# A graph network's gathers: row-by-row loads for one tile of every eighth step instead of every fourth

## The reference

```python
src, dst = (edge_index[0], edge_index[1])
h = node_features @ enc_W + enc_b
for l in range(N_LAYERS):
    cat = jnp.concatenate([h[src], h[dst], edge_features], axis=-1)
    m = jax.nn.relu(cat @ msg_W1[l] + msg_b1[l]) @ msg_W2[l] + msg_b2[l]
    agg = jax.ops.segment_sum(m, dst, num_segments=n_nodes)
    h = _gru_cell(agg, h, gru_Wih[l], gru_Whh[l], gru_bih[l], gru_bhh[l])
return jax.nn.relu(h @ ro_W1 + ro_b1) @ ro_W2 + ro_b2
```

## Time and profile before

| | |
|---|---|
| device time, median of 3 plain runs | 6155.57 us (6152.11 to 6167.82) |
| span of the one profiled execution | 9775.6 us |
| instructions recorded in it | 72,182 |
| granted TensorE clock, mean | 0.571 |
| GpSimd busy | 4639.2 us, 47% of the span |
| VectorE busy | 3532.6 us, 36% |
| TensorE busy (matmuls) | 2880.1 us, 29% |
| ScalarE busy | 346.4 us, 4% |

### The profile page before, as it was taken

How to read it: one execution, slowest core, us unless ns; L and a number is a source line. 1 busy time by engine, 2 the same in 40 slices (tenths; PEclk the granted TensorE clock), 3 DMA queues, 4 the chain that set the end, 5 groups by cost and what they waited for, 6 DMA issues and landing times.

```text
span 9775.6 us, 72182 instructions
## 1 busy us (share of the span) xinstructions
PE 2880.1 (29%) x7290; PEld 1610.2 (16%) x7290; DVE 3532.6 (36%) x4656; ACT 346.4 (4%) x542; POOL 4639.2 (47%) x4865
## 2 busy tenths in 40 slices
PE   3323322322322332222222222223232222322223
PEld 2111111111111221111111111112111111111112
DVE  2333333333333433333333333333333334333334
ACT  0000000000000000000000000000000000000001
POOL 5444444444444454444444444445454445545543
PEclk6555555555555555555555555555555555555555
DMA  3111111111111111111111111111111111111111
GB/s 87 31 31 30 30 30 30 28 31 30 31 30 30 30 28 30 30 30 30 30 30 29 30 30 27 30 31 30 30 31 31 30 30 34 31 31 31 31 30 25
DMA packets 351443, 308.63 MB, mean 32 GB/s; under 512 B 149364, under 2 KB 237518, under 8 KB 350568
## 3 DMA queue, kind: packets, MB, share of 16 engines
q0 software_dynamic: 155328, 159.79, 8.6%
q1 hardware_dynamic: 118271, 110.17, 4.0%
q10 hardware_dynamic: 77328, 33.96, 1.4%
HBM read 280.52 MB, written 22.83 MB: 31 GB/s over the span
## 4 chain that ended last, share of the span: by engine, by line
SPq 57%; issue 38%; DVE 2%; PE 1%; another core or an unknown queue 1%; DMA 0%; ACT 0%; POOL 0%; DVEq 0%; ACTq 0%; POOLq 0%
SPq L473 46%; SPq L469 6%; SPq L642 2%; SPq L633 1%; SPq L527 1%; DVE work_ps L1493 1%; SPq L630 1%; DVE folds L1528 0%; DVE p_src L1490 0%; PE bank L838 0%; DMA p_src<-p_tab 0%; PE work_ps L949 0%; PE bank L962 0%; SPq L662 0%
## 5 line engine op out<-in xcount | busy, mean ns | idle before, releaser
L798 POOL DMA_INDIRECT p_src<-p_tab,idx_all x4767 | 4551.1, 955 | 4916.8 <-DVE work_ps L1493 3467.4
L962 PE MATMUL bank<-hot,folds 128*128 128x96 f32 x2496 | 660.1, 413 | 4012.9 <-issue 2053.0
L1490 DVE TENSOR_TENSOR p_src<-work_ps,p_src 128x512 f32<-128x512 f32 x624 | 427.6, 685 | 3374.9 <-DMA p_src<-p_tab 2912.1
L962 PEld LDWEIGHTS bank<-hot,folds 128*128 128x128 f32 x2496 | 532.1, 296 | 4278.5 <-issue 2198.0
L949 PE MATMUL work_ps<-w_edges,msg 128*128 128x512 f32 x1248 | 1120.0, 997 | 21.4 <-DMA windows_sb<-q_tab 21.4
L1523 DVE SCALAR_TENSOR_TENSOR work_ps<-work_ps,rel 128x1024 f32<-128x1024 f32 x624 | 768.8, 1232 | 21.5
L1493 DVE TENSOR_TENSOR work_ps<-p_src,bank 128x1024 f32<-128x1024 f32 x624 | 767.0, 1229 | 21.4
L1528 DVE TENSOR_REDUCE folds<-work_ps 128x256 f32<-128x1024 f32 x624 | 758.4, 1215 | 0.0
L959 PE MATMUL bank<-hot,counts 128*34 128x96 bf16 x416 | 68.9, 261 | 2248.6 <-issue 1278.6
L1538 DVE TENSOR_TENSOR sums<-bank,sums 128x96 f32 x624 | 158.1, 253 | 872.6 <-remote 699.5
L959 PEld LDWEIGHTS bank<-hot,counts 128*34 128x34 bf16 x416 | 27.1, 108 | 2368.2 <-issue 1359.8
(11 more groups left out here) (167 smaller groups left out, 1800.9 us busy)
## 6 DMA issues: line engine op xcount, KB each, us to landing
p_src<-p_tab ACTq DMA_DIRECT2D x9792, 0.2 KB
p_src<-p_tab SPq DMA_DIRECT2D x9792, 0.2 KB
p_src<-p_tab,idx_all POOLq DMA_INDIRECT x4830
msg<-in_edge_k SPq DMA_DIRECT2D x156, 256.0 KB
pick<-rel_tab SPq DMA_DIRECT2D x312, 96.0 KB
windows_sb<-q_tab ACTq DMA_DIRECT2D x312, 24.0 KB
windows_sb<-q_tab SPq DMA_DIRECT2D x312, 24.0 KB
pick<-q_tab ACTq DMA_DIRECT2D x312, 24.0 KB
```

The costliest lines, as they stand in the source:

```text
L798: pool.indirect_dma_start(out=p_src[r][0:rows, t, :], out_offset=None, in_=p_tab[l][0:NODES, :], in_offset=bass.IndirectOffsetOnAxis(ap=id ...
L962: last = nc.tensor.matmul(fold_ps, folds[:, b, :], hot_all[n % 2][:, s * BLOCKS + b, 1:WINDOW + 1], start=(b == 0), stop=(b == BLOCKS - 1))
L1490: nc.vector.tensor_tensor(rows, edge_ps[k % 2], rows, ALU.add).then_inc(with_edge, 1)
```

## The change

The singles are now the eighth tile of every eighth step, 25 in a layer instead of 51; GpSimd gathers the other 26. SyncE issues 32 of the 64 rows ahead of the inputs of one group and the other 32 ahead of the next group's, each in two loads of sixteen offsets. ScalarE issues pieces of eight rows, each with its own load of eight offsets, from six steps ahead (two pieces) to one step ahead of the tile's own. The landing semaphores are two for each queue instead of four. The list of single nodes and its offsets shrink from 52 to 26 rows.

```diff
-PIECES = 4
-AHEAD_OF = 5
+PERIOD = 2 * GROUP
+PIECES = 8
+AHEAD_OF = 6
 PIECE = (128 - SP_ROWS) // PIECES
-SINGLE_SEMS = 4
-SINGLES = GROUPS - 1
+SINGLE_SEMS = 2
+SINGLES = STEPS // PERIOD - 1
...
         def has_singles(m):
-            return m % GROUP == GROUP - 1 and m // GROUP < SINGLES
+            return m % PERIOD == PERIOD - 1 and m // PERIOD < SINGLES
...
         def single_rows(eng, kind, l, m, first, n, landed):
-            for at in range(first, first + n, PIECE):
-                here = offsets[m // GROUP:m // GROUP + 1, at:at + PIECE]
+            each = min(n, 16)
+            for at in range(first, first + n, each):
+                here = offsets[m // PERIOD:m // PERIOD + 1, at:at + each]
...
         def pieces_at(m):
-            due = [(m + AHEAD_OF - q, q) for q in range(PIECES)]
-            if m == 0:
-                due = [(GROUP - 1, q) for q in range(PIECES) if GROUP - 1 + q <= AHEAD_OF]
+            due = [(m + AHEAD_OF - q * (AHEAD_OF - 1) // (PIECES - 1), q) for q in range(PIECES)]
             return [(at, q) for at, q in due if at < STEPS and has_singles(at)]
...
                     for g in range(2, GROUPS):
-                        single_rows(sp, mybir.EngineType.SP, l, GROUP * (g - 2) + GROUP - 1, 0, SP_ROWS, sp_singles)
+                        half = g % 2 * SP_ROWS // 2
+                        if has_singles((g // 2 - 1) * PERIOD + PERIOD - 1):
+                            single_rows(sp, mybir.EngineType.SP, l, (g // 2 - 1) * PERIOD + PERIOD - 1, half, SP_ROWS // 2, sp_singles)
                         group_inputs(n0 + g, g)
...
-                    single_rows(sp, mybir.EngineType.SP, l, STEPS - 1 - GROUP, 0, SP_ROWS, sp_singles)
...
-        "src_single": src[GROUP - 1::GROUP, BLOCKS - 1, :, RUN - 1],
+        "src_single": src[PERIOD - 1::PERIOD, BLOCKS - 1, :, RUN - 1],
```

More of the change, by code:

```diff
@@ L191, in build @@
         both = pre_all[:].rearrange("p s g f -> p (s g f)")
-        raw_nodes = zr[0:GROUPS, 0:128].bitcast(I32)
-        offsets = p_src[ROW_SLOTS].rearrange("p t f -> p (t f)")[0:GROUPS, 0:128].bitcast(I32)
+        raw_nodes = zr[0:SINGLES + 1, 0:128].bitcast(I32)
+        offsets = p_src[ROW_SLOTS].rearrange("p t f -> p (t f)")[0:SINGLES + 1, 0:128].bitcast(I32)
         src_seen = [dst_flat[:, 0:STEP], both[0:LATE_ROWS, :].bitcast(I32)]
@@ L476, in pieces_at @@
         def pieces_at(m):
-            due = [(m + AHEAD_OF - q, q) for q in range(PIECES)]
-            if m == 0:
-                due = [(GROUP - 1, q) for q in range(PIECES) if GROUP - 1 + q <= AHEAD_OF]
+            due = [(m + AHEAD_OF - q * (AHEAD_OF - 1) // (PIECES - 1), q) for q in range(PIECES)]
             return [(at, q) for at, q in due if at < STEPS and has_singles(at)]
         def nth_single(l, m):
-            return l * SINGLES + m // GROUP
+            return l * SINGLES + m // PERIOD
         def chunk_stages(m):
```

## The result

The changed kernel takes 6250.04 us (median of 4 runs, 6249.08 to 6251.08), the kernel before 6155.17 us (its three runs from ahead of the change and one more): a ratio of 1.0151 with a 95% interval from 1.0137 to 1.0165. It is 94.9 us slower, as forecast (6252), inside the range (6219 to 6262).

A forecast was written before the change was run, and what follows sets the result against it. GpSimd's gathers were taken to bound the kernel, with next to no row wait in plain runs. 6155.6 us plus 96.5 us for 77 added gathers, all other parts 0, gave 6252 us (+1.57%), range 6219 to 6262 us.

The forecast's parts named there:

- The term of 96.5 us: GpSimd's uninterrupted stream: 77 of the 78 tiles handed back become gathers at 1.2537 us each, 96.5 us more.
- The whole plain run as a GpSimd sum: GpSimd over the whole kernel before: head, gathers, layer starts and tail, without row waits, sum to 6179.5 us.
- the head's wait: Step 3, in the head: GpSimd's 13.61 us wait for stored tables covers one added gather, cost 0.
- 59% was added by profiling: SyncE's and ScalarE's queues: recording their instructions stretches the 6155.57 us plain run to a 9775.6 us span.
- the group sums 31.7 and 33.4: Clean work for a group of four steps: SyncE 31.7 us, ScalarE 33.4 us, both below GpSimd's 39.0 us.
- Rival 1: SyncE's and ScalarE's row queues bound plain runs too; change faster, 1365 us off, 4790 us; chance 0.04.
- Rival 2: GpSimd bounds, but its 32.51 us stall for step 3's rows is real: 6220 us; chance 0.04.
- Rival 3: GpSimd has idle time in plain runs that takes the added gathers: no change, 6156 us; chance 0.03.
- Rival 4: ScalarE's last row piece late by 6.7 us each time, VectorE without lead: 503 us more, 6755 us; chance 0.02.
- Rival 5: Row transfers hold back the DMA engines; 9,984 fewer give 5873 to 6138 us; chance 0.01.
- Row pieces: ScalarE's eight pieces, one load and eight rows each, take 4.3 us; last has 3 us cover; cost 0.
- What would show it: 4,908 gathers at 1.25 to 1.26 us, 4,800 rows a queue, slot waits nearly gone, GpSimd chain, span 6250 to 6900 us.

The follow-up runs named there:

- second job: Kind A session; kernel before 6154.97 us, changed kernel 6250.75 us, no row tiles 6344.55 us, two gathers less a step 5275.24 us.
- kind B: Sessions on one chip in which the kernel before, unedited, takes 9756 to 9811 us.
- kind A: Sessions on one chip in which the kernel before, unedited, takes about 6155 us.
- the old split: Changed kernel with SyncE's 64 rows in one burst and ScalarE's in four pieces of sixteen: 6253.3 us, 1.0161 of the kernel before.
- first job: Kernel before 9756.0 us; without row tiles 7604.8, one gather less a step 8930.5, two less 8117.0; changed kernel with two less 6770.3 us.
- the third: Kernel before 9810.8 us; 96 rows on SyncE 12046.4, six more row tiles a layer 10135.0, eight more 10263.4, changed kernel 8156.7 us.

## Why the prediction was right, and where it was not

- *GpSimd sets the end in the plain runs, and 78 more gathers are what the change costs.* Right for the kind of job that it was timed in: shown by three gather counts on one line (second job), and by a chain that is GpSimd's own. The term of 96.5 us measured 94.9 and 95.8.
- *The whole plain run as a GpSimd sum.* The sum came out at 6179.5 us for 6155.6, and nearly all its surplus is in rows taken from a trace of kind B. The changed kernel's head ends at 83.2 us with one gather more, not at 95.1; the waits at the two layer starts are 5.7 us and next to none, not 12.1; the gathers keep 1.257 us, not 1.2587. Only the tail was right: counted from the end of the last gather's pitch, as in the sum, it is 6247.3 - 6215.5 - 1.3 = 30.5 us, not 30.0. The fit put all of the surplus into the pitch, which made 1.2537 us too low. With the head's wait gone no gather is free, so the term should have been 78 x 1.257 = 98.0 us instead of 96.5. The measured 95 is some 3 us less: the kernel before takes 6154.97 us where the one without rows less 153 pitches gives 6152.2. A small row wait in the kernel before would do that, and so would the wait at layer 1's start, 5.1 us in the trace without rows and 5.7 to 7.6 us in those with rows; it stays open.
- *59% was added by profiling, the surplus is the cost of recording.* Wrong. This is the step that failed: the kernel before takes 9756 and 9811 us in plain timed runs on kind B, and the changed kernel's profiled span on kind A is its time. By its span, the profile shown of before was taken in one kind of job and the times in the other. What rested on the clean stretches of that trace (rows at 0.318 and 0.338 us, the group sums 31.7 and 33.4) survived roughly, since these stretches run at kind A's pace: 64 rows with their loads take 25.0 us for the 26.7 of the sum, and SyncE's group 30.3 us for 31.7. The forecast was right because the plain times were weighed above the trace's span, and because the changed kernel was then timed in a job of the same kind. The second was luck: on kind B the same change gains 17%, outside the range and with the other sign.
- *Rival 1, the row queues bound.* It had 4 chances in 100 and is the truth on kind B. Its condition was misplaced: it was to decide by a pitch below 1.233 us, but GpSimd keeps its 0.95 us and 0.30 us gap on both kinds (0.95 in each gather row shown). It is the row queues that get slower.
- *Rival 2, a real stall at the first row tile.* Not on kind A. The whole difference left is 3 us, not 32.5, and the kernel with two gathers less, which up to step 7 issues what the kernel before issues, shows it directly: SyncE issues step 3's rows from 86.54 us for 25.04 us, not from 140.68 for 43.08, and GpSimd has no wait above 0.32 us from there until 259 us.

```profile
86.54 25.04 SPq L473 DMA_DIRECT2D p_src<-p_tab  x64
```

- *Rival 3, idle time in GpSimd,* is out by the same line of counts. *Rival 4, a late last piece on ScalarE:* no wait of VectorE is on rows in the changed kernel's trace, and the old split gives the same time. *Rival 5, small transfers on the DMA engines:* with GpSimd as bound, 9,984 fewer transfers gained nothing. A row is two packets, not the one of the sum: queue q10 falls from 77,328 to 67,344, by 9,984 for 4,992 rows. And the sentence on the Trainium skill there leaves out the condition of its section, high HBM utilization, which DMA engines busy for 1 tenth do not suggest.
- *Row pieces.* ScalarE's load of eight offsets takes 819 ns at the median, where the sum took the 1.23 us of sixteen, so a piece is some 3.9 us, not 4.3. It was hidden anyway.
- *What would show it.* Gathers 4,908, rows 4,800 a queue, the chain at GpSimd, waits for slots gone, and a span below 6900 us: all as written for kind A. The span fell because the job was of the other kind, not because fewer rows were recorded. On kind B the changed kernel's GpSimd still waits 1768.6 us for slots, the sign that the prediction named for being wrong.

## What to carry to other kernels

When a profiled span and the plain times disagree by more than a few per cent, do not explain the gap by profiling: first see whether the same kernel's plain time in the job of the profile is the span. And before work is moved between issuing queues, write down each queue's clean time a group beside the bound's (39.0 against 31.7 and 33.4 here): the move pays only while the receiving side has room, and how much room it has can differ from job to job, and from layer to layer. A cut of the bound's own work, such as two gathers a step left out, measures the next bound at once.

## What the runs showed of the hardware

- The same kernel takes 6155 us in some jobs and 9756 to 9811 us in others. In the latter SyncE's and ScalarE's queues step from instruction to instruction at about 0.70 us during stretches, even where the instruction is a register move of 29 ns. Over the trace of before, SyncE's stretches begin 4 to 6 us after a burst of GpSimd's indirect gathers starts and end some 4 us after it stops; ScalarE's begin some 9 us after the start. Counted so, they follow the gathers; whether the gathers' traffic causes them wasn't tried on its own.
- What makes a job kind A or kind B stays open. The records number the chips: 1 in the first job (B), 4 in the second (A) and 4 in the third (B). So either one chip can be of both kinds at different times, or the number stands for chips of different hosts; nothing here decides it, and "a slow chip" isn't shown.
- GpSimd's gather keeps its pitch on either kind, 1.257 us on kind A and 1.257 to 1.260 on kind B, with no row transfers beside it or with as many as 14,688 on SyncE's queue.
- Which of two schedules is better turned over with the kind: 1.0151 on kind A, 0.832 on kind B.
